# Two adaLN layers with ALiBi attention and mixtures of experts: weights sent in pieces, tile tables and padding moved ahead of a stage boundary, both modulations computed together, and a new order for the uses of a shared PSUM bank

## The chip, the cores and the metric

One core of a Trainium2 chip runs the whole program in one launch. The metric is device time in microseconds, the median over runs. The times stand below beside the profile.

## What is computed

The input is x of shape (32, 256, 128): 32 batch elements of 256 tokens. Each of two layers has its own modulation and then does attention and a mixture of experts. Cut to what matters:

```python
for layer in (0, 1):
    mod = (silu(c) @ wmod).reshape(32, 6, 1, 128)       # c: (32,128), wmod: (128,768)
    sa, ca, ga, sb, cb, gb = mod                        # ga, gb: at least 0.25 in size
    h = layernorm(x) * (1 + ca) + sa
    x = x + ga * attention(h)                           # 16 heads of 8 columns, 256 x 256
    h = layernorm(x) * (1 + cb) + sb
    x = x + gb * experts(h)                             # 8 experts, 128 -> 512 -> 128
# layer 0: attention with a distance bias; top-2 of 8 experts, relu
# layer 1: attention(LN(h)) + LN(h); RMS norm, top-1 of 8 experts, silu, biases b1 and b2
```

Only the chosen experts are computed: tokens are gathered by expert into a buffer in HBM, and each expert's region is worked through in tiles.

## The kernel before, in words

The program is a row of blocks with a barrier over all engines between them: the setup (from L265), `attention(l=0)`, `experts(l=0)`, `attention(l=1)`, `experts(l=1)`. Inside a block every engine has its own instruction list, and semaphores order the engines. SP is the engine that issues the DMAs.

**Setup.** SP issues 24 loads one after another (L293), cT and the two wmod last; then, once VectorE has zeroed the two `stack` buffers (L333), rows of constants into `stack` (L296). ScalarE waits for all loads and takes exp (L312); VectorE finishes silu (L351 to L353); TensorE multiplies (L321, 323, 325). One buffer `mod_sb` holds the rows of one layer's modulation: VectorE shapes layer 0's (L360 to L375), SP writes it to HBM (L299), and only then do TensorE (`if l: pe.wait_ge(moded, 8)`) and VectorE (`dve.wait_ge(mod_out, 16)`) go on with layer 1's. Last SP writes rows of the gates (L301, L303).

**Attention.** `run_ticks` makes 40 ticks; a tick works on several batch elements at once, `at(off)` giving the element that is `off` ahead of or behind the tick's own. In a tick TensorE makes 16 passes `a_pass(h)` of scores for the row maximum (L1173; VectorE takes the maximum, L923, from one of two buffers A), eight `chunk(c)` of scores (L1200, and L1203 in layer 0) for ScalarE's exp (L753), and four `weigh` of probabilities by values (L1218). The second set of scores has the negated row maximum as rows of `stack`: TensorE turns it (`turn_max`, L1180, two halves of eight heads), ScalarE copies it (`max_rows`, L746), SP's DMA puts it into `stack` (`stack_max`, L542). The maximum of half 0 is used from chunk 0 of the next tick, that of half 1 from its chunk 4.

Between these passes TensorE makes small products that share one PSUM bank, M0: `turn_h2` (L1140), `gate` (L1236), `turn_max` (two), `project_v` (L1162), the turns of `On`, `yT` and `xn` (L1140), `project_out` (L1231), and every second tick `count` (L1243, L1246), after which VectorE's `place` gives each token a slot in its expert's region (to L1056) and POOL scatters the tokens (L640). Each use waits (`m0_read`) until the reader of the use before it has read. The order is written out by hand in each engine's `tick`. Ticks with `place` alternate with ticks in which the expert is chosen.

SP sends an attention block's weights for the experts, w1 and w2 (2 MB each, and the biases in layer 1), as whole DMAs ahead of all ticks (L591). In layer 1 `load_front` (L504 to L508) loads the middle x, the experts' outputs and modulation rows, and POOL adds them up (L612).

**Experts.** First SP pads: the tail of the gathered buffer (L1385), then, when VectorE has copied the regions' fill `run` to integers (L1447), eight pads, each at an address read from `run_i` (L1389, L1390). Meanwhile VectorE builds the tables of the tiles (to L1471). When the pads have landed and the table is there, SP loads the first tile (`load_tile`, L1396 and L1399), TensorE turns it (`turn_x`, L1611), and the two products follow (L1620, L1629). Results are scattered by POOL (L1433, L1430).

These lines order one tick of TensorE around `turn_max` before the change:

```python
chunk(2)
a_pass(6)
if at(-1):
    m0_read((logits_read, -3), (h_ready, 1), (mT_read, -1, 1))
    turn_max(*at(-1), 1)
heads_step(weigh, -1, 0)
...
a_pass(15)
if at(0):
    ...
    turn_max(*at(0), 0)
chunk(7)
```

Of the kernel before, what the change touches and what calls it, by code (L numbers as in the profile page):

```python
# [9 lines left out]
ALU = mybir.AluOpType  # L10
AX = mybir.AxisListType

P = 128
# [5 lines left out]
H, HD = 16, 8  # L19
# [114 lines left out]
def build(nc, a, out):  # L134
    with ExitStack() as ctx:
# [6 lines left out]
        def dram(name, shape, dt=F32):  # L142
# [135 lines left out]
            (ln_cols[:, :], a["ln_cols"]), (wv_id[:, :], a["wv_id"]), (gate_w[:, :, :], a["gate_w"]), (cT[:, :, :], a["cT"]),  # L278
            (wmod[:, 0, :], a["wmod0"]), (wmod[:, 1, :], a["wmod1"]),
# [3 lines left out]
        loaded, ready, modp, moded, mod_out = (sem(n) for n in  # L283
            ("setup_loaded", "setup_ready", "setup_products", "setup_modulation", "mod_rows_written"))
        stack_zero, stack_loaded = sem("setup_stack_zeroed"), sem("setup_stack_loaded")
# [3 lines left out]
        with nc.Block() as block:  # L289
            @block.sync  # L290
            def _(sp):
                for dst, src in loads:
                    sp.dma_start(dst, src).then_inc(loaded, 16)  # L293
# [7 lines left out]
                sp.dma_start(gate_rows[:, D:2 * D], mod_sb[:, GA * D:(GA + 1) * D]).then_inc(gates_out, 16)  # L301
                for f in range(2):
                    sp.dma_start(gate_rows[:, f * (D // 2):(f + 1) * (D // 2)].rearrange("b (h d) -> b h d", d=HD),  # L303
                                 mod_sb[:, GA * D:(GA + 1) * D].rearrange("b (h f d) -> b f h d", f=2, d=HD)[:, f, :, :])\
                        .then_inc(gates_out, 16)
                sp.wait_ge(gates_out, 48)
# [3 lines left out]
            def _(act):  # L310
                act.wait_ge(loaded, 16 * len(loads))
# [3 lines left out]
            def _(pe):  # L315
                pe.wait_ge(ready, 1)
                for l in range(2):
                    if l:
                        pe.wait_ge(moded, 8)
                    for j in range(6):  # L320
                        pe.matmul(M0[:, j * B:(j + 1) * B], wmod[:, l, j * D:(j + 1) * D], silu[:, l, :],  # L321
                                  start=True, stop=True)
                    pe.matmul(A[0][0:B, :, :].rearrange("p t s -> p (t s)"), silu[:, l, :], wmod[:, l, 0:512],
                              start=True, stop=True)
                    pe.matmul(A[1][0:B, 0, :], silu[:, l, :], wmod[:, l, 512:768], start=True, stop=True)\
                        .then_inc(modp, 1)
                pe.matmul(M1[:, 0:1], wo[:, :], vo_bias[:, 0:1], start=True, stop=True).then_inc(modp, 1)
# [1402 lines left out]
```

## Time and profile before

| | us |
|---|---|
| median of 3 runs | 2106.24 |
| lowest and highest | 2105.88 and 2109.68 |
| profiled execution, its own time | 2108.88 |
| span of the profiled execution, first to last instruction | 2107.1 |
| mean granted TensorE clock, share of full | 0.923 |

The span falls into these stages, by the barriers in the trace:

| stage | us |
|---|---|
| setup | 0 to 44.9 |
| attention, layer 0 | 44.9 to 795.6 |
| experts, layer 0 | 795.6 to 1095.2 |
| attention, layer 1 | 1095.2 to 1901.8 |
| experts, layer 1 | 1901.8 to 2107.1 |

How to read it: PE is TensorE's products, PEld its weight loads, DVE is VectorE, ACT ScalarE, POOL GpSimd, SPq the queue of SyncE. In a row of the timeline the numbers are the start and the duration in us, and in brackets stands the engine's idle time before the instruction and who ended it. In a row by lines stand the count, the busy time in us, the mean of one in ns, and the idle time before them by what ended it.

### The profile page before, as it was taken

The page shows a single profiled execution, that of the slowest core. Times are in us where ns is not written, and L with a number is a line of the kernel's source. Part 1 is how long each engine was busy: PE and PEld are TensorE (multiplying, and loading weights), DVE is VectorE, ACT ScalarE, POOL GpSimd, SP SyncE. Part 2 cuts the span into 40 slices and gives each one's busy share as a digit, 9 for nine tenths or more (in the row PEclk, how much of TensorE's full clock was granted, in tenths as well). Part 3 has the DMA queues.
Part 4 walks back from the last instruction along what each step waited for, and adds up shares of the span by engine and source line. Part 5 has one row for each costly group of instructions (what it writes and reads, how often), then busy time and mean ns, then how long its engine had stood idle before and what let it go on. Part 6 is the DMA issues. An engine that isn't in the chain of part 4 may idle for free. (4 is left out here: it accounts for less than half of the span.)

```text
span 2107.1 us, 43953 instructions
## 1 busy us (share of the span) xinstructions
PE 1613.4 (77%) x14050; PEld 1155.9 (55%) x14050; DVE 1494.7 (71%) x4845; ACT 1137.7 (54%) x2198; POOL 667.5 (32%) x740
## 2 busy tenths in 40 slices
PE   2488888888888845999963777877877877843996
PEld 1266565656566624999951444444544444523886
DVE  4478888888888734777744787788888788833664
ACT  0277777777677631222211676666666666641543
POOL 0011323232323252555531223233333333230544
PEclk9899999999999977999985898899999999976998
DMA  3333343333333313222235445455455545415443
GB/s 106 85 69 69 79 79 77 79 76 80 77 79 79 67 39 83 72 72 74 72 104 126 85 95 122 97 108 119 102 108 113 109 101 110 91 59 169 133 125 81
DMA packets 267612, 193.24 MB, mean 92 GB/s; under 512 B 26111, under 2 KB 257441, under 8 KB 266612
## 3 DMA queue, kind: packets, MB, share of 16 engines
q1 hardware_dynamic: 252024, 155.41, 35.2%
q0 software_dynamic: 15360, 35.03, 5.4%
q8 instruction: 114, 1.87, 0.4%
q14 instruction: 114, 0.93, 0.2%
HBM read 95.34 MB, written 53.18 MB: 70 GB/s over the span
## 5 line engine op out<-in xcount | busy, mean ns | idle before, releaser
L923 DVE TENSOR_REDUCE mx<-A 128x2 f32<-128x512 f32 x1024 | 688.4, 682 | 213.7 <-PE A L1173 197.3
L753 ACT ACTIVATE probs<-B 128x1024 f32<-128x1024 f32 x512 | 521.8, 1019 | 281.1 <-PE B L1200 154.6
L1173 PE MATMUL A<-stack 126*128 126x256 bf16 x2048 | 398.3, 284 | 113.4 <-DVE mx L923 92.3
L1200 PE MATMUL B<-stack 128*128 128x256 bf16 x2048 | 367.0, 282 | 67.4 <-DMA stack<-mrow 66.7
L1173 PEld LDWEIGHTS A<-stack 126*128 126x128 bf16 x2048 | 169.6, 100 | 266.8 <-DVE mx L923 165.4
L1218 PE MATMUL M<-probs,vals 128*32 128x256 f32 x4096 | 295.1, 408 | 23.8 <-DVE On L946 19.7
L1200 PEld LDWEIGHTS B<-stack 128*128 128x128 bf16 x2048 | 199.4, 102 | 122.3 <-DMA stack<-mrow 82.0
L640 POOL DMA_INDIRECT gathered<-h,slot_in x192 | 186.9, 974 | 128.6 <-DVE slot_in L1056 82.3
L1629 PE MATMUL A<-w2s,hid 128*128 128x128 f32 x1792 | 219.5, 276 | 8.5 <-issue 8.5
L604 POOL TENSOR_TENSOR parts<-rem,parts 128x512 bf16<-128x512 f32 x64 | 74.5, 1165 | 468.1 <-ACT parts L732 468.1
L1629 PEld LDWEIGHTS A<-w2s,hid 128*128 128x128 f32 x1792 | 208.8, 192 | 12.9 <-issue 11.8
L1620 PE MATMUL B<-xtT,w1s 128*128 128x256 f32 x896 | 205.1, 382 | 0.0
L1433 POOL DMA_INDIRECT expert_out<-yt,row_dest x144 | 141.9, 986 | 156.9 <-DVE yt L1536 122.1
L1578 ACT ACTIVATE hid<-B 128x1024 f32<-128x1024 f32 x72 | 73.8, 1025 | 211.8 <-PE B L1620 211.8
L1218 PEld LDWEIGHTS M<-probs,vals 128*32 128x32 f32 x4096 | 120.5, 114 | 116.6 <-issue 75.3
L1203 PE MATMUL B<-dist,slope_ident 128*128 128x128 bf16 x1024 | 183.4, 219 | 0.0
L1620 PEld LDWEIGHTS B<-xtT,w1s 128*128 128x128 f32 x896 | 167.9, 192 | 20.9
L626 POOL TENSOR_TENSOR h<-xn,back_rows 128x256 f32<-128x256 f32 x64 | 46.5, 726 | 366.2 <-ACT xn L691 366.2
L1430 POOL DMA_INDIRECT out<-yt,row_dest x80 | 78.8, 985 | 126.4 <-DVE yt L1533 108.2
L1478 DVE TENSOR_SCALAR w1s<-w 128x512 f32 x112 | 55.5, 495 | 76.2 <-PE B L1620 68.4
L1611 PE MATMUL M<-ident,xt 128*128 128x128 f32 x224 | 43.9, 279 | 81.1 <-DMA xt<-gathered 81.1
L671 ACT ACTIVATE rs<-mv,eps_col 128x2 f32<-128x2 f32 x192 | 55.6, 290 | 93.1 <-DVE mv L849 62.2
(182 smaller groups left out, 2405.5 us busy)
## 6 DMA issues: line engine op xcount, KB each, us to landing
stack<-parts SPq DMA_DIRECT2D x768, 64.0 KB
xt<-gathered SPq DMA_DIRECT2D x112, 132.0 KB, 2.2
probs<-gathered SPq DMA_DIRECT2D x40, 256.0 KB
w<-in_w SPq DMA_DIRECT2D x4, 2048.0 KB, 10.1
back_rows<-mod_rows SPq DMA_DIRECT2D x64, 128.0 KB, 3.7
x_mid<-X SPq DMA_DIRECT2D x64, 128.0 KB, 2.9
hid<-expert_out SPq DMA_DIRECT2D x64, 128.0 KB
X<-in_x SPq DMA_DIRECT2D x32, 128.0 KB, 3.8
```

The source lines that it names most:

```text
L604: pool.tensor_tensor(parts[u][:, :, 2, :], rem[:, :, :], parts[u][:, :, 1, :], ALU.subtract)\
L640: pool.indirect_dma_start(gathered[l], bass.IndirectOffsetOnAxis(ap=place, axis=0), (h3 if l else h2)[:, v, t, :], None).then_inc(scat_out ...
L753: act.activation(probs[c % 4][:, :, :, :], Bp[BUFFER[c]][:, :, :, :], ACT.Exp, scale=EXP_SCALE[l][c // 4]).then_inc(b_exp.handle, 1)
L923: dve.tensor_reduce(mx[u][:, h, :], A[h % 2][:, :, :], AX.X, ALU.max).then_inc(a_max.handle, 1)
L1173: ins = pe.matmul(A[h % 2][:, t, :], stack[u][0:n, h, 0, t * P:(t + 1) * P], stack[u][0:n, h, 1, :], start=True, stop=True)
L1200: ins = pe.matmul(Bp[BUFFER[c]][:, j, t, :], stack[u][:, h, 1, t * P:(t + 1) * P], stack[u][:, h, 0, :], start=True, stop=(l == 1))
L1203: ins = pe.matmul(Bp[BUFFER[c]][:, j, t, t * P:(t + 1) * P], slope_ident[:, h % HH, :], dist[:, :], start=False, stop=True)
L1218: ins = pe.matmul(M1[VW * j:VW * j + VW, 0:S], vals[u][:, t, first:first + VW], probs[(2 * g + j // 2) % 4][:, j % 2, t, :], start=(q == 0 ...
L1430: ins = pool.indirect_dma_start(expert_out[l], dest, yt[s % HELD][:, t, :], None, bounds_check=B * S - 1, oob_is_err=False)
L1433: ins = pool.indirect_dma_start(expert_out[l], dest, yt[s % HELD][:, t, :], None)
L1620: ins = pe.matmul(dst[:, f, :], w1s[u][:, f * P:(f + 1) * P], xtT[u][:, :], start=True, stop=True)
L1629: ins = pe.matmul(A[u][:, t, 0:D], hid[u][:, f, t * P:(t + 1) * P], w2s[u][:, f, :], start=(f == 0), stop=(f == FC - 1))
```

## The change

It does five things.

1. In the setup cT and both wmod are loaded first, with a semaphore of their own; both layers' products, rows and columns have their own places, so that the second waits for nothing of the first; silu stands ahead of VectorE's wait for all loads; POOL instead of VectorE zeroes `stack`.
2. The weights are cut by expert into 16 pieces (18 with the biases), of which SP sends one at the end of each tick from `at(-2)` on.
3. The padding and the tables of the tiles move from the start of the experts' block to the end of the attention block's lists of SP and VectorE. The waits for the table go.
4. `load_front` moves from the end of SP's tick to its start and waits for `h_stats` instead of `h_rows`.
5. The uses of M0 in a tick, and with them steps of ScalarE and VectorE, get a new order: `turn_max` of half 1 stands right behind chunk 0, that of half 0 behind a_pass 10 (layer 1) or a_pass 12 and a turn of heads (layer 0), `project_v` ahead of chunk 3, `count` behind chunk 6, `place` behind the maximum of pass 14.

The diff, cut; first the setup, the weights, the padding and the tables:

```diff
+        first_loads = [(cT[:, :, :], a["cT"]), (wmod[:, 0, :], a["wmod0"]), (wmod[:, 1, :], a["wmod1"])]
+        mods = [mod_sb[:, :], hid[0][0:B, 0:3, :].rearrange("b c s -> b (c s)")]
+        mod_cols = [M0[:, 0:6 * B], M1[:, 0:6 * B]]
...
             def _(sp):
+                for dst, src in first_loads:
+                    sp.dma_start(dst, src).then_inc(first_loaded, 16)
                 for dst, src in loads:
                     sp.dma_start(dst, src).then_inc(loaded, 16)
                 sp.wait_ge(stack_zero, 2)
...
-                    sp.dma_start(mod_rows[l], mod_sb[:, :]).then_inc(mod_out, 16)
-                    sp.wait_ge(mod_out, 16 * (l + 1))
+                    sp.dma_start(mod_rows[l], mods[l]).then_inc(mod_out, 16)
...
-                act.wait_ge(loaded, 16 * len(loads))
+                act.wait_ge(first_loaded, 16 * len(first_loads))
...
-                    if l:
-                        pe.wait_ge(moded, 8)
...
+            @block.gpsimd
+            def _(pool):
+                for u in range(2):
+                    pool.memset(stack[u][:, :, :, :], 0.0).then_inc(stack_zero, 1)
...
-                for u in range(2):
-                    dve.memset(stack[u][:, :, :, :], 0.0).then_inc(stack_zero, 1)
...
-                    dve.wait_ge(modp, l + 1)
-                    if l:
-                        dve.wait_ge(mod_out, 16)
+                    dve.wait_ge(modp, 3 if l else 1)
...
-                    sp.wait_ge(h_rows.handle, h_rows.after(b - 2))
+                    sp.wait_ge(h_stats.handle, h_stats.after(b - 2))
...
-            weights = [(w1[:, :, :], a[f"w1_{l}"]), (w2[:, :, :, :], a[f"w2_{l}"])]
+            weights = [piece for e in range(E) for piece in
+                       ((w1[:, e, :], a[f"w1_{l}"][:, e, :]), (w2[:, e, :, :], a[f"w2_{l}"][:, e, :, :]))]
...
             def tick(at):
+                if l and at(3):
+                    load_front(*at(3))
                 if at(0):
                     stack_up(*at(0), 1)
...
-            for dst, src in weights:
-                sp.dma_start(dst, src).then_inc(weights_in, 16)
+                if at(-2):
+                    for dst, src in itertools.islice(more_weights, 1):
+                        sp.dma_start(dst, src).then_inc(weights_in, 16)
             run_ticks(tick)
...
+                         pads[E:PADS]).then_inc(padded, 16)
+            sp.wait_ge(run_ready, 1)
+            for e in range(E):
+                r = sp.value_load(run_i[0:1, e:e + 1], min_val=e * REGION, max_val=(e + 1) * REGION - TOK)
+                sp.dma_start(gathered[l][bass.ds(r, TOK), :], pads[e]).then_inc(padded, 16)
+            sp.wait_ge(padded, 16 * (E + 1))
             sp.wait_ge(weights_in, 16 * len(weights))
```

ScalarE's and VectorE's order in a tick, and what is added behind VectorE's ticks:

```diff
                 chunk(0)
+                step(max_rows, -1, 1)
...
-                step(max_rows, -1, 1)
                 step(mid_part, 1)
+                step(values, 0)
                 chunk(3)
-                step(values, 0)
...
                 chunk(5)
+                step(max_rows, 0, 0)
...
-                step(max_rows, 0, 0)
                 chunk(7)
...
                 rows(1, rms_moments, -2)
+                maxima(14, 1)
                 group(l, place, -4)
-                maxima(14, 1)
...
             run_ticks(tick)
+            dve.tensor_copy(run_i[:, :], run[:, :]).then_inc(run_ready, 1)
...
```

TensorE's order in a tick:

```diff
                 chunk(0)
+                if at(-1):
+                    m0_read((h_ready, 1), (mT_read, -1, 1))
+                    if not at(1):
+                        counted_before()
+                    turn_max(*at(-1), 1)
                 a_pass(2)
                 heads_step(weigh, -2, 3)
                 if at(-3):
-                    m0_read((h_ready, 1), (mT_read, -1, 1), (mT_read, -2, 2))
+                    m0_read((mT_read, -1, 2), (logits_read, -4))
...
-                if at(-1):
-                    m0_read((logits_read, -3), (h_ready, 1), (mT_read, -1, 1))
-                    turn_max(*at(-1), 1)
                 heads_step(weigh, -1, 0)
                 a_pass(7)
+                if at(0):
+                    m0_read((logits_read, -3), (mT_read, -1, 2), (h_ready, 1))
+                    project_v(*at(0))
                 chunk(3)
-                if at(0):
-                    m0_read((mT_read, -1, 2), (h_ready, 1))
-                    project_v(*at(0))
...
                 a_pass(10)
+                if l:
+                    turn_first_max()
...
                 heads_step(turn_heads, -1, 0)
-                if group_done(at, -4):
...
-                    count(*at(-4))
+                if l == 0:
+                    turn_first_max()
                 a_pass(13)
                 chunk(6)
+                if group_done(at, -4):
+                    m0_read((mT_read, 0, 1), *[(x1_ready, -2)] * (l == 0), (logits_read, -3))
+                    count(*at(-4))
...
                 a_pass(15)
-                if at(0):
-                    ...
-                    turn_max(*at(0), 0)
                 chunk(7)
                 if at(2):
-                    m0_read((mT_read, 0, 1), (h_ready, 1))
+                    if group_done(at, -4):
+                        pe.wait_ge(pos_read.handle, pos_read.after(at(-4)[1]))
+                    else:
+                        m0_read((mT_read, 0, 1), (h_ready, 1))
                     turn(by_tile(xn[at(2)[2]]), xn_ready, at(2)[0], xn_T)
```

In the experts' block the copy of `run`, the tables, the padding and these waits go:

```diff
-            sp.wait_ge(table_ready, 1)
-            sp.wait_ge(zeroed, 16 * (E + 1))
...
-            act.wait_ge(table_ready, 1)
...
-            pe.wait_ge(table_ready, 1)
```

## Rows read from the trace of the kernel before

**Rows 1.** Windows, two attention loops: us; busy us of PE, PEld, DVE, ACT, POOL; PEclk; DMA; GB/s.

```profile
79.20:742.60 663.40, 575.27 (x5958) 396.38 (x5957) 545.25 (x1517) 463.59 (x870) 181.19 (x196) 0.99 0.39 74
1139.60:1852.40 712.80, 554.28 (x4786) 330.14 (x4784) 580.96 (x1812) 471.03 (x958) 217.56 (x264) 0.91 0.50 103
```

**Rows 2.** Timeline of the setup.

```profile
1.67 3.47 DVE L333 MEMSET stack<- 128x4096 uint32 x1 [1.67 <-PEq L1723]
...
16.96 0.26 ACT L312 ACTIVATE silu<-cT 128x64 f32<-128x64 f32 x1 [14.94 <-DMA wmod<-in_wmod]
...
18.54 2.77 PE L321 MATMUL M<-silu,wmod 128*128 128x32 f32 x12 [18.54 <-DVE silu L353]
...
24.04 0.36 DVE L360 COPY modT<-M 128x192 f32<-128x192 f32 x1 [5.56 <-PE A L325]
...
29.45 2.77 PE L321 MATMUL M<-silu,wmod 128*128 128x32 f32 x12 [5.44 <-DVE mod_sb L375]
...
40.02 0.28 DVE L375 SCALAR_TENSOR_TENSOR mod_sb<-mod_sb,qk 32x128 f32<-32x128 f32 x1
...
42.51 0.92 SPq L303 DMA_DIRECT2D gate_rows<-mod_sb  x2
```

**Rows 3.** The page's DMA issues: KB each, us from issue to landing.

```profile
w<-in_w SPq DMA_DIRECT2D x4, 2048.0 KB, 10.1
...
X<-in_x SPq DMA_DIRECT2D x32, 128.0 KB, 3.8
```

**Rows 4.** Timeline, the starts of the two attention blocks.

```profile
59.77 0.49 DVE L858 BATCH_NORM_STATS2 st<-X 128x6 f32<-128x128 f32 x2 [19.12 <-DMA X<-in_x]
...
1114.95 0.72 POOL L612 TENSOR_TENSOR hid<-hid 128x256 f32<-128x256 f32 x1 [25.23 <-DMA gb_row<-mod_rows]
```

**Rows 5.** Timeline, the two boundaries from attention to experts.

```profile
811.43 3.57 SPq L1399 DMA_DIRECT2D xt<-gathered  x3
...
813.78 0.66 PE L1611 MATMUL M<-ident,xt 128*128 128x128 f32 x2 [38.99 <-DMA xt<-gathered]
...
1887.28 0.17 DVE L1056 CAST slot_in<-r 128x4 int32<-128x4 f32 x1
...
1903.96 9.60 SPq L1390 DMA_DIRECT2D gathered<-in_pads  x8
...
1927.20 0.66 PE L1611 MATMUL M<-ident,xt 128*128 128x128 f32 x2 [41.20 <-DMA xt<-gathered]
```

**Rows 6.** PE by lines, 450.7 to 701.5: twelve ticks of layer 0.

```profile
L1200 PE MATMUL B<-stack 128*128 128x256 bf16 x385 | 74.2, 273 | 6.2 <-DMA stack<-mrow 6.2
L1180 PE MATMUL M<-ident_b,mneg 128*16 128x128 bf16 x48 | 6.7, 221 | 3.2 <-DVE lg L1002 3.2
L1140 PE MATMUL M<-ident,On 128*128 128x128 f32 x24 | 5.3, 301 | 8.0 <-ACT vals L739 8.0
```

**Rows 7.** PE by lines, 1449.5 to 1813.5: sixteen ticks of layer 1.

```profile
L1200 PE MATMUL B<-stack 128*128 128x256 bf16 x512 | 83.2, 288 | 21.6 <-DMA stack<-mrow 21.6
L1180 PE MATMUL M<-ident_b,mneg 128*16 128x128 bf16 x64 | 9.2, 228 | 13.8 <-DVE lg L1002 8.6 <-DVE run L1048 5.2
```

**Rows 8.** Windows: two neighbouring ticks of layer 0, two of layer 1.

```profile
492.50:512.00 19.50, 17.99 (x191) 12.57 (x189) 17.25 (x53) 13.84 (x27) 5.96 (x8) 1.00 0.43 81
512.00:534.30 22.30, 18.64 (x198) 12.89 (x197) 17.71 (x49) 16.25 (x31) 7.05 (x8) 1.00 0.36 76
1586.50:1611.00 24.50, 19.93 (x152) 11.50 (x152) 17.77 (x58) 14.57 (x30) 7.48 (x9) 0.80 0.44 106
1611.00:1631.90 20.90, 16.33 (x159) 10.14 (x157) 18.11 (x59) 15.68 (x33) 6.06 (x8) 1.00 0.51 94
```

**Rows 9.** Timeline of POOL and of DVE around 521.9.

```profile
521.81 1.15 POOL L604 TENSOR_TENSOR parts<-rem,parts 128x512 bf16<-128x512 f32 x1 [5.16 <-ACT parts L732]
...
521.88 1.11 DVE L930 TENSOR_SCALAR mneg<-mx 128x16 bf16<-128x16 f32 x1
```

**Rows 10.** Durations of L930 over the span: ns min, median, max.

```profile
L930 DVE TENSOR_SCALAR mneg<-mx x128: 160/175/1148, 86.7 to 1852.5; 128x16 bf16<-128x16 f32 x128
```

More of the change, by code:

```diff
@@ L1 @@
+import itertools
 from contextlib import ExitStack
@@ L343, in _ @@
                 ch.mark(dve.memset(ones_col[:, :, :], 1.0))
+                dve.wait_ge(set_act, 1)
+                ch.link(dve.tensor_scalar(silu[:, :, :], silu[:, :, :], 1.0, None, ALU.add))
+                ch.link(dve.reciprocal(silu[:, :, :], silu[:, :, :]))
+                dve.tensor_tensor(silu[:, :, :], silu[:, :, :], cT[:, :, :], ALU.mult).then_inc(ready, 1)
                 ch.mark(dve.memset(h3[:, :, :, :], 0.0))
@@ L426, in attention @@
         "gb_row ones_col Y expert_out XR a w1 w2 b1 b2".split())
+    tile_iota, run_i, cnt_i, n_tiles, tile_base, reached, tile_tab, tile_e, tile_row, tile_rev = (g[n] for n in
+        "tile_iota run_i cnt_i n_tiles tile_base reached tile_tab tile_e tile_row tile_rev".split())
+    slots = SLOTS[l]
     n_choice = CHOICES[l]
@@ L439, in attention @@
     weights_in, lin_in = sem("weights_in"), sem("lin_in")
+    run_ready, padded = sem("run_ready"), sem("slack_padded")
     def transfers(name, dmas, begun=1, n=2):
@@ L560, in _ @@
                     sp.dma_start(stack[u][BROW:BROW + 2 * NB, :, 0, :], a["no_rows"].bitcast(BF16)).then_inc(lin_in, 16)
+            more_weights = iter(weights)
             for t in (x_in, stack_in, m_in, x1_out, front_in, back_in, x2_out, x2_in, ga_in, gate_in):
@@ L1272, in heads_step, with counted_before, turn_first_max @@
                         step(*at(off), g)
+                def counted_before():
+                    if group_done(at, -5):
+                        pe.wait_ge(pos_read.handle, pos_read.after(at(-5)[1]))
+                def turn_first_max():
+                    if at(0):
+                        m0_read(*[(x1_ready, -2)] * (l == 0), (base_ready if l else v_ready, 0))
+                        turn_max(*at(0), 0)
                 a_pass(0, 1)
                 chunk(0)
+                if at(-1):
[3 more added lines that the diff above has]
+                    turn_max(*at(-1), 1)
                 a_pass(2)
@@ L1278, in tick @@
                 if at(-3):
-                    m0_read((h_ready, 1), (mT_read, -1, 1), (mT_read, -2, 2))
-                    if not at(-1) and group_done(at, -5):
-                        pe.wait_ge(pos_read.handle, pos_read.after(at(-5)[1]))
+                    m0_read((mT_read, -1, 2), (logits_read, -4))
+                    if not at(-1):
+                        counted_before()
                     turn_h2(*held(at, -3))
@@ L1326, in tick @@
                 a_pass(15)
-                if at(0):
+                chunk(7)
+                if at(2):
                     if group_done(at, -4):
```

110 lines of the change are left out of this document (46 added, 64 removed).

## Prediction

> **What bounds the kernel now.** I read the stages first, from the barriers: of 2107.1 us the two attention loops take 663.4 and 712.8 us [rows 1], the experts' loops most of the rest, and around the barriers lie stretches in which the compute engines have next to nothing to do. Then I read the timeline of each such stretch, and last the idle time of TensorE by lines inside the loops.
>
> The setup is one chain: silu starts at 16.96 because it waits for wmod, loaded last; layer 0's products start at 18.54, VectorE's part at 24.04; layer 1's products only at 29.45, their last vector step ends at 40.30, and the gate rows leave at 42.51 [rows 2]. The attention blocks start with VectorE and POOL waiting 19.12 and 25.23 us for their first input [rows 4], the experts' with TensorE waiting 39 and 41 us for the first tile [rows 5].
>
> In the loops no single engine is full. In layer 0 TensorE is busy 18.64 of a 22.30 us tick and VectorE 17.71; in the tick without `place` it is 17.99 and 17.25 of 19.50, so there the two hardly wait. In layer 1 it is 19.93 and 17.77 of 24.50, 16.33 and 18.11 of 20.90 [rows 8]. What is lost are waits of TensorE in its written order: for the row maximum coming back by DMA, for the shared bank's readers, for `vals` [rows 6, 7]. TensorE's granted clock is 0.99 in layer 0's loop, 0.91 in layer 1's [rows 1] and 0.80 in the long tick shown [rows 8]: layer 1, where TensorE waits more, spends part of its time at 1.2 GHz, not 2.4.
>
> **The change part by part.** Gains are negative; the bounds stand in brackets.
>
> *Setup.* With cT and wmod first, three issues take about 1.4 us (0.46 each, the two gate rows' pair [rows 2]). Their landing before: wmod was issued about 12 us in and silu began at 16.96, so 4.9 us; now silu can start near 7.1 and the products 1.6 later, near 8.7. Both layers' products, 5.5 us each (18.54 to 24.04), are done near 19.7. VectorE still waits for all loads (16.96), does 0.7 us of other work, and needs 5.4 us for each layer (24.04 to about 29.4): it ends near 28.5 instead of 40.30. The three gate writes no longer wait for a landing and end near 30.0 instead of 43.4. That is −13.4. POOL's zeroing of `stack` is an operation that this trace doesn't show. VectorE takes 3.47 us for 4096 words [rows 2]; POOL takes 1.15 us for 512 elements of a two-input sum [rows 9], 2.25 ns each, which gives 9.2 us for a buffer, or 18.4 if it goes by two-byte elements. For two buffers that is 7 to 37 us, behind which all of SP's writes queue. Up to 18 us it hides behind the modulation; at 37 SP's nine last issues would end near 43, where they end now. I take −12 [−13.5 to 0].
>
> *First attention block's start.* X was queued behind 4 MB of weights; 2 MB takes 10.1 us to land, X itself 3.8 [rows 3]. Without the weights, X is issued in the block's first microsecond, near 45.5, and VectorE starts at about 49.3 instead of 59.77 [rows 4]: −10.5 [−9.4 to −11]. The pieces are 256 KB, an eighth of 10.1 us or 1.3 us each, one per tick behind `stack_max`. DMA is busy 0.39 and 0.50 of the loops [rows 1], and the next transfer that TensorE waits for comes most of a tick later, so I cost them at 0; were each on the path, 34 pieces would cost 44 us.
>
> *Second attention block's start.* POOL's first sum waits for gb_row, the last of `load_front`'s DMAs, until 1114.95 [rows 4]. Without the weights, SP's first dozen issues at 0.46 us end near 1101 and land 3.8 us later, near 1105: −10 [−8 to −12]. Moving `load_front` to the head of the tick puts it ahead of `stack_up`; `h_stats` comes before `h_rows`, so SP should not stand longer: 0.
>
> *Experts' starts.* Before, tail pad, run copy, eight pads, their landing and then the tile. Now SP starts with `load_tile`. From its issue to TensorE took 2.35 us (811.43 to 813.78 [rows 5]), reading an address about 0.7 (9.60/8 less an issue of 0.46), and SP's first instruction stands some 0.4 behind the barrier. Layer 0: 795.6 + 3.5 = 799.1 instead of 813.78, −14.7 [−13 to −15]. Layer 1: 1905.2 instead of 1927.20, −22. There the moved work may show: the last `place` ends at 1887.45, the eight pads take 9.6 us to issue [rows 5], land by about 1900 to 1901, and the old block's barrier was at 1901.8. The new wait (`padded`) has nothing behind it on SP but the block's end, so it costs 0 to 4; I take −21 [−22 to −17]. In layer 0 TensorE had its last work 38.99 us ahead of 813.78, at 774.8 [rows 5], 21 us ahead of the barrier at 795.6; behind it stands one `place`, and the rest covers some 6 us of tables and 12 of pads.
>
> *Layer 0's loop.* In the twelve ticks TensorE waited 6.2 us for the maximum's DMA, 3.2 at `turn_max` and 8.0 at `On` [rows 6]: 17.4 in six pairs of ticks, 2.9 a pair. Half 0's `turn_max` moves up three to four passes of some 1.2 us, half 1's five; both maxima then land well ahead of their chunks. ScalarE's `values` moves up too, but behind `mid_part`, so the wait for `vals` goes only in part. New waits are `turn_h2` on the second half's copy, the turn of xn on `pos_read`, and `project_v` one chunk earlier; behind each stands TensorE's whole list, and VectorE and ScalarE live on its passes. I bound each by 0 to 0.6 us per tick, about the present wait at `On` (8.0/12). In the tick without `place` VectorE has 2.2 us of slack in all, mostly at the tick's start, and gains little. I take half of 2.9, less a little: −1.3 a pair, times 15.9 pairs (663.4/41.8 [rows 1, 8]), −21 [−8, `turn_max`'s 3.2 alone, to −32].
>
> *Layer 1's loop.* In sixteen ticks 21.6 us for the maximum's DMA and 13.8 at `turn_max` [rows 7], 35.4 in eight pairs or 4.4; with smaller waits at the turns of heads and xn about 5.2, and 15.7 pairs make −82. If the pair only comes down to VectorE's busy time plus the slack that layer 0 has (41.8 − 34.96 = 6.84 [rows 8]), it is 35.88 + 6.84 = 42.7 instead of 45.4, −2.7 or −42. I take the middle, −62 [−28, `turn_max`'s wait alone, to −88]. This includes some of the clock: less waiting means less time at the low level.
>
> The sum: 12 + 10.5 + 21 + 14.7 + 10 + 62 + 21 = 151. The profiled execution took 2108.88, of which 2107.1 is its span and 1.8 lies around it; it is 2.6 above the median 2106.24. Against itself the sum gives 1957.7, against the median 1955. The ends of the sum are 2023 (83 gained) and 1913 (193 gained).
>
> **The rivals.**
> *The loops don't move.* The waits go but TensorE's next one is for VectorE's maxima, busy 17 to 18 us of every tick [rows 8]. Only the boundaries are left: 12 + 10.5 + 14.7 + 10 + 21 = 68, time 2038. Against it: the long ticks leave VectorE 4.6 and 6.7 us of slack. 10%.
>
> *POOL's zeroing stands in VectorE's way.* At 521.81 a POOL instruction of 1.15 us ran; a VectorE step that began 0.07 us later took 1.11 us [rows 9], against a median of 0.175 [rows 10], and both ended within 0.03 us. So an instruction of this kind can be held by POOL. If silu's steps in the setup are held so by a zeroing of 9 to 18 us, the setup's gain goes, time 1967. The Trainium skill ("SBUF — State Buffer", section "Who interferes with whom") has the mechanism: the two engines share a pair of ports as an exclusive lock, held for the whole instruction, and the other "fully blocks"; it also says that a VectorE operation of one input outside the two-port modes is not touched, which is why this stays a rival. By that rule, the row of 1.11 us is the first case. 8%.
>
> *The starts don't do what they say.* The pieces or pads collide with transfers that the loop needs, or new waits hold the block's ends: half of the boundary gain of 56 at the four starts goes, and 10 more is lost in the loops: 1993. 6%.
>
> *Slower: the shared bank becomes the chain.* The new order puts `turn_max` of half 1, `turn_h2`, `gate` and `project_v` close behind each other at the start of the tick, each waiting for a reader on another engine. A wait of the kind at `On` costs 0.67 us; four of them in each of 31.5 ticks of two loops are 2.7 × 63 = 169, and with the boundaries' 68 the time is 2207. It decides from 68/63 = 1.1 us per tick, two such waits that nothing covers. For it: nine uses of one bank in 21 us. Against it: passes and chunks of 1.2 us stand between the uses, and the bank's waits that there are now come to 0.9 us a tick in each layer (3.2 + 8.0 over twelve, 13.8 over sixteen [rows 6, 7]). 3%.
>
> **How the numbers follow.** Forecast 73%, the rivals 10, 8, 6 and 3. The predicted time is 1955. The range is 1915 to 2025: the sum's ends, which take in the second and third rival; the first and the fourth lie above it. Faster by over 0.2% (4 us, about what a measurement of this kernel can tell from no change): 0.96; within it 0.01; slower 0.03.
>
> **What would show it.** Right: products at about 9 us and the barrier near 32; VectorE's first statistics 4 to 5 us behind that; TensorE's first turn 3.5 us behind each experts' barrier; L1200's wait for mrow and L1180's idle time near zero; the granted clock of layer 1's loop above 0.91. Wrong: L1180 or the turn of h2 waiting for ScalarE; xn's turn waiting for `run` in each second tick; VectorE's idle time in the long ticks unchanged; a last block end held by pads; a POOL zeroing that outlasts 30 us.

## The result, and the profile after

The changed kernel takes 1957.28 us (1955.88 to 1961.96, four runs) against 2106.49; the ratio is 0.9293, 95% interval 0.9274 to 0.9311. The forecast was 1955. The profiled execution has a span of 1956.3 us, 150.8 less than before.

ScalarE loads a table at the start of every block, a mark that stands in each trace. From mark to mark (the last stage to the end of the span), in us:

| kernel | setup to | attention 0 | experts 0 | attention 1 | experts 1 |
|---|---|---|---|---|---|
| before | 46.0 | 749.8 | 300.7 | 805.5 | 205.1 |
| changed | 36.6 | 710.2 | 285.4 | 740.3 | 183.8 |
| difference | -9.4 | -39.6 | -15.3 | -65.2 | -21.3 |

Setup of the changed kernel, timeline (start, duration, engine, line; in brackets the idle time before):

```profile
0.75 13.79 POOL L338 MEMSET stack<- 128x8192 bf16 x2 [0.29 <-POOLq L1739]
...
5.74 0.26 ACT L320 ACTIVATE silu<-cT 128x64 f32<-128x64 f32 x1 [3.71 <-DMA wmod<-in_wmod]
6.03 8.55 DVE L354 TENSOR_SCALAR silu<-silu 128x64 f32<-128x64 f32 x1 [2.51 <-ACT silu L320]
...
15.48 2.77 PE L327 MATMUL M<-silu,wmod 128*128 128x32 f32 x12 [15.48 <-DVE silu L356]
...
20.88 2.77 PE L327 MATMUL M<-silu,wmod 128*128 128x32 f32 x12
...
33.01 0.93 SPq L310 DMA_DIRECT2D gate_rows<-hid  x2
```

ScalarE starts 11.2 us earlier than in [rows 2] and both layers' products run back to back. But the first VectorE step of silu, 128x64 numbers, took 8.55 us: it ended at 14.58 with POOL's second zeroing at 14.54. So the gate rows leave at 33.01 instead of 42.51.

The starts of the two attention and the two experts' blocks, timeline:

```profile
39.22 0.49 DVE L877 BATCH_NORM_STATS2 st<-X 128x6 f32<-128x128 f32 x2 [6.70 <-DMA X<-in_x]
...
750.00 0.69 PE L1627 MATMUL M<-ident,xt 128*128 128x128 f32 x2 [25.20 <-DMA xt<-gathered]
...
1039.53 0.72 POOL L631 TENSOR_TENSOR hid<-hid 128x256 f32<-128x256 f32 x1 [13.90 <-DMA gb_row<-mod_rows]
...
1775.71 0.69 PE L1627 MATMUL M<-ident,xt 128*128 128x128 f32 x2 [23.72 <-DMA xt<-gathered]
```

Against [rows 4, 5] the idle time ahead of these is 12.4, 13.8, 11.3 and 17.5 us shorter.

One pair of ticks in each loop, by windows (columns as in [rows 1]):

```profile
333.00:373.00 40.00, 36.76 (x385) 25.49 (x385) 34.59 (x100) 29.69 (x58) 13.03 (x15) 1.00 0.54 95
1517.80:1559.50 41.70, 33.44 (x309) 21.05 (x309) 37.56 (x119) 30.52 (x64) 14.99 (x18) 0.96 0.59 121
```

The pairs in [rows 8] took 41.8 and 45.4 us with the same work; now 40.0 and 41.7. Over the sixteen ticks of [rows 7] and those shown below, a pair of layer 1 went from 45.5 (364.0 / 8) to 42.1 us (336.8 / 8). The granted clock of layer 1's pair is 0.96, against 0.80 and 1.00 in the two ticks of [rows 8]. PE by lines, first twelve ticks of layer 0 (333 to 573.5):

```profile
L1246 PE MATMUL B<-stack 128*128 128x256 bf16 x384 | 73.8, 272 | 0.3 <-ACT probs L772 0.3
...
L1226 PE MATMUL M<-ident_b,mneg 128*16 128x128 bf16 x48 | 6.7, 221 | 1.5 <-ACT hT L733 1.5
...
L1186 PE MATMUL M<-ident,On 128*128 128x128 f32 x24 | 5.3, 300 | 0.0
```

and sixteen ticks of layer 1 (1348.5 to 1685.3):

```profile
L1246 PE MATMUL B<-stack 128*128 128x256 bf16 x512 | 80.6, 281 | 0.2 <-DMA stack<-mrow 0.2
...
L1264 PE MATMUL M<-probs,vals 128*32 128x256 f32 x1024 | 75.8, 412 | 16.6 <-DVE On L965 16.6
...
L1226 PE MATMUL M<-ident_b,mneg 128*16 128x128 bf16 x64 | 8.9, 221 | 3.8 <-ACT hT L733 3.3
...
L1186 PE MATMUL M<-ident,xn 128*128 128x128 f32 x32 | 6.9, 299 | 10.6 <-DVE xn L882 10.5
```

The waits of [rows 6, 7] are gone or small. In layer 1 two others grew: at the turn of xn, in each second tick, from 3.3 us in the sixteen ticks before to 10.6, and at `weigh` from 7.0 to 16.6.

### The profile page after: what moved, and what is told of

The parts are those of the page before. It is cut to its first block and busy times, and to the rows that moved or that the text cites. A ratio compares the mean times of both kernels' runs of the same rounds, so it can differ in the third digit from the quotient of the medians.

```text
span 1956.3 us, 43980 instructions
## 1 busy us (share of the span) xinstructions
PE 1580.6 (81%) x14050; PEld 1151.8 (59%) x14050; DVE 1492.6 (76%) x4843; ACT 1129.0 (58%) x2198; POOL 684.3 (35%) x742
## 5 line engine op out<-in xcount | busy, mean ns | idle before, releaser
L1246 PE MATMUL B<-stack 128*128 128x256 bf16 x2048 | 357.4, 277 | 4.4 <-DMA stack<-mrow 2.8
L1219 PEld LDWEIGHTS A<-stack 126*128 126x128 bf16 x2048 | 160.0, 99 | 288.8 <-DVE mx L942 182.6
L1264 PE MATMUL M<-probs,vals 128*32 128x256 f32 x4096 | 285.5, 395 | 41.6 <-DVE On L965 36.4
L1246 PEld LDWEIGHTS B<-stack 128*128 128x128 bf16 x2048 | 203.8, 101 | 38.9 <-DMA stack<-mrow 4.1
L1249 PE MATMUL B<-dist,slope_ident 128*128 128x128 bf16 x1024 | 183.3, 219 | 0.0
L1599 ACT ACTIVATE hid<-B,b 128x256 f32<-128x256 f32 x160 | 62.8, 475 | 76.6 <-PE B L1636 73.8
L1249 PEld LDWEIGHTS B<-dist,slope_ident 128*128 128x128 bf16 x1024 | 100.3, 98 | 2.7
```

The source lines that it names most:

```text
L1219: ins = pe.matmul(A[h % 2][:, t, :], stack[u][0:n, h, 0, t * P:(t + 1) * P], stack[u][0:n, h, 1, :], start=True, stop=True)
L1246: ins = pe.matmul(Bp[BUFFER[c]][:, j, t, :], stack[u][:, h, 1, t * P:(t + 1) * P], stack[u][:, h, 0, :], start=True, stop=(l == 1))
L1249: ins = pe.matmul(Bp[BUFFER[c]][:, j, t, t * P:(t + 1) * P], slope_ident[:, h % HH, :], dist[:, :], start=False, stop=True)
L1264: ins = pe.matmul(M1[VW * j:VW * j + VW, 0:S], vals[u][:, t, first:first + VW], probs[(2 * g + j // 2) % 4][:, j % 2, t, :], start=(q == 0 ...
```

## The experiments

Twelve kernels ran. All are the changed kernel with one edit, unless it says otherwise. From mark to mark:

| kernel | median | setup to | attention 0 | experts 0 | attention 1 | experts 1 |
|---|---|---|---|---|---|---|
| undo_setup | 1974.60 | 45.1 | 709.2 | 286.6 | 745.9 | 183.3 |
| undo_weights | 1976.37 | 29.8 | 720.5 | 286.7 | 755.0 | 183.8 |
| undo_pads | 1989.44 | 36.7 | 709.5 | 301.3 | 743.1 | 205.6 |
| undo_order | 2029.30 | 29.7 | 741.2 | 286.9 | 781.2 | 183.1 |
| pool_words | 1953.95 | 29.6 | 710.5 | 286.8 | 742.6 | 183.5 |
| front_only | 2092.77 | 45.5 | 748.4 | 301.2 | 786.5 | 205.9 |
| late_max0 | 2033.78 | 29.2 | 740.8 | 286.6 | 789.0 | 183.9 |
| late_max1 | 1948.03 | 29.1 | 711.7 | 285.5 | 737.7 | 183.6 |
| after_again | 1955.28 | 36.6 | 710.4 | 286.3 | 743.4 | 183.9 |
| pads_two | 1959.80 | 29.2 | 710.0 | 286.7 | 748.0 | 183.6 |
| best | 1948.17 | 29.9 | 710.6 | 285.4 | 736.9 | 183.5 |
| half0_only | 2093.62 | 45.4 | 731.4 | 301.0 | 804.9 | 205.5 |

Layer 1's attention varies by itself: 740 to 746 us in kernels that are the same there. Each row of marks is one execution; the medians are over four or five. The expectations below take the setup's end of the changed kernel at the next block's first instruction, 36.4, against the barrier, 44.9, of before; by the mark the difference is 9.4, not 8.5.

**undo_setup:** the setup's code as in before (all of the first part of the diff).

```diff
-                act.wait_ge(first_loaded, 16 * len(first_loads))
+                act.wait_ge(loaded, 16 * len(loads))
...
+                    if l:
+                        pe.wait_ge(moded, 8)
...
-                    pool.memset(stack[u][:, :, :, :], 0.0).then_inc(stack_zero, 1)
...
+                    dve.memset(stack[u][:, :, :, :], 0.0).then_inc(stack_zero, 1)
...
+                    if l:
+                        dve.wait_ge(mod_out, 16)
```

> The changed kernel with the setup as it was before (loads last, one buffer of rows, VectorE zeroing). The stages in the trace of the changed kernel say that the setup's barrier came at 36.4 instead of 44.9: this run should take 8.5 us more than the changed kernel, 1966, if the setup's end is what the first attention block starts from. The rival, that the block's start has slack of its own (its X, or the landing of the rows in stack), gives less than 4 us.

Measured: 1974.60, ratio to before 0.9361 (0.9317 to 0.9406), 17 above the changed kernel. The setup is 8.5 us longer and nothing behind it gives that back; of the rest 5.6 stand in layer 1's attention, which the edit doesn't touch and which lies in its spread.

**undo_weights:** two whole DMAs ahead of the ticks.

```diff
+            weights = [(w1[:, :, :], a[f"w1_{l}"]), (w2[:, :, :, :], a[f"w2_{l}"])]
+            for dst, src in weights:
+                sp.dma_start(dst, src).then_inc(weights_in, 16)
             run_ticks(tick)
```

> The changed kernel with the weights sent whole ahead of the ticks, as before. From the stages: VectorE's first statistics stood 14.9 us behind the barrier and stand 2.8 now, POOL's first sum in layer 1 19.8 and 8.7 now: 12.0 + 11.1 = 23 us, so 1980. The rival, that the 34 pieces cost the loops something that this run gets back (up to 1.3 us each), gives 23 less up to 44, so 1936 to 1978, and shorter steady ticks than the changed kernel's 40.0 and 42.1 us a pair.

Measured: 1976.37, ratio 0.9376 (0.9327 to 0.9426). The attention blocks take 10.3 and 14.7 us more, 25 in all; the setup came out 6.8 us shorter in this execution (see after_again). From the mark to VectorE's first statistics it is 13.9 us instead of 2.7, and to POOL's first sum in layer 1 18.7 instead of 7.4: 11.2 and 11.3, so some 3 of layer 1's 14.7 are its spread. The pairs are 40.0 and about 42.1, as in the changed kernel: the pieces cost the loops nothing.

**undo_pads:** padding and tables back at the start of the experts' block.

```diff
-            sp.wait_ge(padded, 16 * (E + 1))
...
+            sp.wait_ge(table_ready, 1)
+            sp.wait_ge(zeroed, 16 * (E + 1))
```

> The changed kernel with padding and tables of the tiles at the start of the experts' blocks, as before. The first turn of a tile stood 18.2 and 25.4 us behind the barriers and stands 3.5 and 3.4 now, 36.7 in all; SP's wait for the pads (4.3 us) holds the end of layer 1's attention block 4.6 us longer now. Theory: 32 us more than the changed kernel, 1989, and a block end 14.3 us behind the last place in layer 1 instead of 18.9. The rival, that the block's late end has another cause than the pads: 37 us more, and 18.9 stays.

Measured: 1989.44, ratio 0.9425 (0.9378 to 0.9473), 32 above: experts' blocks 15.9 and 21.8 longer. In layer 1 the mark of the next block stands 14.5 us behind the last `place`, not 19.3. So the moved pads do hold that block's end; how is under pads_two.

**undo_order:** TensorE's, ScalarE's and VectorE's order of before.

> The changed kernel with the uses of the shared bank, and ScalarE's and VectorE's steps, in the order of before. By the stages the loops got 28.5 and 58.7 us shorter: if that is all of the new order's doing, this run takes 87 us more, 2044, with pairs of ticks of 41.8 and 45.5 us, TensorE waiting about 0.5 and 1.35 us a tick for the maximum's DMA, and a granted clock of about 0.91 in layer 1's loop. The rival, that the earlier load_front or the weights in pieces did part of it in layer 1: a pair there below 45.5, and less than 75 us more.

```diff
+                if at(-1):
+                    turn_max(*at(-1), 1)
                 heads_step(weigh, -1, 0)
...
                 a_pass(15)
+                if at(0):
+                    turn_max(*at(0), 0)
                 chunk(7)
```

Measured: 2029.30, ratio 0.9631 (0.9582 to 0.9680), 72 above. By the marks 31 us more stand in layer 0, pairs 41.8, the whole gain of that loop, and 41 in layer 1, pairs 44.4 on average and not 45.5, with a setup 6.9 shorter. The rival holds there: part of layer 1's gain comes from elsewhere. The granted clock of layer 1's loop (1105 to 1783) is 0.95, not the 0.91 expected.

**front_only:** the kernel before, with `load_front` moved.

```diff
-                    sp.wait_ge(h_rows.handle, h_rows.after(b - 2))
+                    sp.wait_ge(h_stats.handle, h_stats.after(b - 2))
...
             def tick(at):
+                if l and at(3):
+                    load_front(*at(3))
```

> The kernel before with nothing but load_front's new place and wait. With the old order of the bank the changed kernel had pairs of ticks of about 44.3 us in layer 1, not 45.5, so some 19 us of layer 1's loop came from elsewhere. In the kernel before, POOL's first sum waited 3.7 us a tick for gb_row, the last of load_front's transfers. Theory A (load_front did it): pairs of about 44.3 us, 2087, POOL's wait for gb_row gone. Theory B (the weights in pieces or the shifted phase of the ticks did it): 2106, pairs of 45.5.

Measured: 2092.77, ratio 0.9940 (0.9919 to 0.9961), which is 8 to 17 us and 13 by the medians; by the profiles 19.0 us in layer 1's attention, pairs 44.3 on average. POOL's waits by line in the kernel before (1449.5 to 1813.5; total us, times, longest):

```profile
POOL parts L604 <- ACT parts L732: 100.0, 16, 8.6
POOL hid L612 <- DMA gb_row<-mod_rows: 59.0, 16, 6.7
```

and in front_only (1437 to 1788):

```profile
POOL parts L604 <- ACT parts L732: 146.0, 16, 12.4
```

In front_only the wait for gb_row is not among POOL's. Theory A holds as far as `load_front`'s move does it, with 13 to 19 us. That POOL's waiting was the cost is not shown: of the 59.0 us, 46.0 came back as a longer wait for `parts`.

**half0_only:** the kernel before, with half 0's turn, its copy and `count` moved.

```diff
                 a_pass(10)
+                if l:
+                    turn_first_max()
...
                 heads_step(turn_heads, -1, 0)
+                if l == 0:
+                    turn_first_max()
...
                 chunk(5)
+                step(max_rows, 0, 0)
```

> The kernel before with one part of the new order alone: half 0's turn_max behind pass 10 or 12, its copy behind chunk 5, count behind chunk 6. Undoing this part in the changed kernel cost 76 us, as much as the whole order (72). Theory (this one move carries the order's gain by itself): 2106 less 65 to 80, 2026 to 2041, with pairs of 40.0 to 40.3 us in layer 0 and no wait for the maximum's DMA. Rival (it needs the other moves, or the earlier load_front in layer 1): layer 0 as said, layer 1's pairs 44 or more, 2055 or more.

Measured: 2093.62, ratio 0.9927 (0.9898 to 0.9956). The rival holds in layer 1: nothing there. In layer 0 it is 18.3 us, of the 28.5 of the changed kernel's loop, with pairs of 40.7 and not 40.0 to 40.3. TensorE's wait for the row maxima (L1173) is 11.6 us in six pairs of layer 0 (450.7 to 694.9), against 9.2 in late_max1, where pairs are 40.2; of the moves that late_max1 has and half0_only lacks, that of `place` behind pass 14 is the one that touches these maxima. It was not run by itself. PE by lines in layer 1 (1447 to 1800):

```profile
L1200 PE MATMUL B<-stack 128*128 128x256 bf16 x492 | 80.0, 288 | 23.9 <-DMA stack<-mrow 23.9
```

and the timeline:

```profile
1587.05 0.36 ACT L746 ACTIVATE mrow<-M 16x256 bf16<-16x256 bf16 x1
...
1590.17 0.33 SPq L507 DMA_DIRECT2D front_rows<-mod_rows  x1
1590.55 0.47 SPq L508 DMA_DIRECT2D gb_row<-mod_rows  x1
1591.07 0.69 SPq L542 DMA_DIRECT2D stack<-mrow  x1
...
1595.09 0.61 PE L1200 MATMUL B<-stack 128*128 128x256 bf16 x4 [1.28 <-DMA stack<-mrow]
...
1612.61 0.43 SPq L508 DMA_DIRECT2D gb_row<-mod_rows  x1
1613.08 0.69 SPq L542 DMA_DIRECT2D stack<-mrow  x1
```

The copy of half 0 is ready at 1587.41, but its DMA leaves at 1591.07, right behind `load_front`'s last one, in SP's order. TensorE waits 23.9 us in some 15.4 ticks, 1.55 a tick, for the maximum, no less than the 1.35 of [rows 7].

**late_max0:** half 0's part late again, and `count` ahead of chunk 6 with it.

```diff
-                if l:
-                    turn_first_max()
...
                 a_pass(15)
+                if at(0):
+                    turn_max(*at(0), 0)
                 chunk(7)
```

> The changed kernel with half 0's turn_max back behind pass 15, ScalarE's copy ahead of chunk 7 again, and count ahead of it: the first half of the maximum is late again. If chunk 0's wait for the maximum's DMA was what half 0 cost, TensorE waits about 1 us at every chunk 0 again in layer 0's long ticks and 1.35 us in layer 1, and the time is 20 to 45 us above the changed kernel's, 1977 to 2000. If VectorE's passes bound the ticks anyway, pairs stay at 40.0 and 42.1 and the time below 1965.

Measured: 2033.78, ratio 0.9664 (0.9633 to 0.9695), 76 above the changed kernel and far above the 1977 to 2000 expected. By the marks 31 us more stand in layer 0 and 43 to 49 in layer 1, against its spread of 740 to 746: as much as the whole order. PE by lines in layer 0 (338 to 590):

```profile
L1246 PE MATMUL B<-stack 128*128 128x256 bf16 x384 | 73.9, 273 | 10.1 <-DMA stack<-mrow 10.1
```

The wait for the maximum's DMA is back, 0.84 us a tick.

**late_max1:** half 1's turn behind pass 6, with the old places of `project_v`, `values` and its copy.

```diff
-                    m0_read((h_ready, 1), (mT_read, -1, 1))
-                    turn_max(*at(-1), 1)
...
                 a_pass(6)
+                if at(-1):
+                    turn_max(*at(-1), 1)
```

> The changed kernel with half 1's turn_max back behind pass 6, and with it turn_h2's old waits, project_v behind chunk 3, ScalarE's copy and values in their old places. If the second half carries the other part of the gain (the old order as a whole cost 72 us), this run and the one with half 0 late add up to it: 27 to 52 us here, 1984 to 2009, with TensorE waiting for vals at the turn of On again in layer 0 (0.67 us a tick). If either half alone gives nearly the whole loss, this run is at 2020 or more; if half 0 carries it all, below 1965.

Measured: 1948.03, ratio 0.9260 (0.9225 to 0.9295). No loss: layer 0 1.6 us longer, layer 1 2.6 to 8 shorter. Most of the 9 us under the changed kernel's median are the setup's, whose mark stands 7.4 us earlier (see after_again). PE by lines, layer 0 (333 to 573):

```profile
L1186 PE MATMUL M<-ident,On 128*128 128x128 f32 x24 | 5.3, 301 | 8.0 <-ACT vals L758 8.0
```

The wait at `On` is back in full, 0.67 us a tick, and the pair is 40.2 instead of 40.0. The two halves don't add up: without half 1's part nothing is lost that can be told from chance, so half 0's part carries the gain, together with what late_max1 leaves in place, the moves of `place` and `load_front`.

**pool_words:** four-byte words.

```diff
-                    pool.memset(stack[u][:, :, :, :], 0.0).then_inc(stack_zero, 1)
+                    pool.memset(stack[u][:, :, :, :].rearrange("p h o s -> p (h o s)").bitcast(F32), 0.0).then_inc(stack_zero, 1)
```

> The changed kernel with one line other: POOL zeroes stack as 4096 four-byte words a buffer instead of 8192 two-byte elements. In the changed kernel's trace the two zeroings take 13.8 us, and silu's first VectorE step ran from 6.03 to 14.58, to their end; in the two runs without the new weights or order the same step ended at 7.72, with the first zeroing, and the setup's barrier came 6.9 us earlier, near 29.5. Theory (POOL's zeroing holds VectorE's step, and its time goes by elements): both zeroings end near 7.7, the step ends there in every execution, the barrier comes near 29.5, and the time is 7 us below a disturbed execution of the changed kernel, 1950 to 1951 against its median of 1957. Rival (the time goes by bytes, or the step waits for something else): the zeroing still takes 13.8 us or the step is as long as before; time 1957.

Measured: 1953.95, ratio 0.9286 (0.9260 to 0.9312); the setup's mark at 29.6.

```profile
0.75 6.96 POOL L338 MEMSET stack<- 128x4096 f32 x2 [0.29 <-POOLq L1739]
...
5.85 1.90 DVE L354 TENSOR_SCALAR silu<-silu 128x64 f32<-128x64 f32 x1 [2.34 <-ACT silu L320]
```

Half the elements, half the time; the step ends with the second zeroing again, now at 7.75. The theory holds for the setup. The time is not the 1950 to 1951 expected: the medians differ by less (3 us) than the marks (7), and the intervals overlap.

**after_again:** no edit.

> The changed kernel once more, nothing edited: beside the kernels of this call, and as a second look at its setup. In its first profile silu's VectorE step ended with POOL's second zeroing (14.58) and the barrier came at 36.4; in three edited kernels that have the same setup it ended with the first zeroing (7.7) and the barrier came near 29.5. Theory (which of the two zeroings lets the step go falls out anew in each execution): 36.4 or 29.5 and nothing between, time 1957 or 1950. Rival (it belongs to the program as built): 36.4 again.

Measured: 1955.28, ratio 0.9260 (0.9232 to 0.9288); the step took 8.67 us and the mark is 36.6, as in the first profile. Six edited kernels with the same two zeroings gave: held to the second zeroing in one (undo_pads), released by the first in undo_weights, undo_order, late_max0, late_max1 and pads_two. Two executions of one program agree, which speaks for the rival; each edited kernel was profiled once. The step's own start doesn't decide: 5.91 to 6.03 where it was held to the second, 5.75 to 6.04 where the first let it go. What in a program does stays open.

**pads_two:** half of the pads from ScalarE's queue.

```diff
+            act.wait_ge(run_ready, 1)
+            pad_regions(act, E // 2, E)
```

> The changed kernel with the eight pads shared: four issued by SP, four by ScalarE, which has no work left there. In the changed kernel SP issues them for 9.7 us from 1754.5 and then waits 4.3 us for their landing; the last scatter was issued at 1758.0 and, by the kernel before (barrier 8.8 us behind the last scatter), would have let the block end near 1767.7. Theory: the barrier comes about 4 us earlier, 14.3 to 15 us behind the last place instead of 18.9, the time falls by 4; layer 0 is unchanged (its scatters end later than its pads). Rival (the landing is bound by the bytes, 388 KB each, not by the issues): no change.

Measured: 1959.80, ratio 0.9286 (0.9259 to 0.9313), no gain on after_again. SP's waits at the end of layer 1's attention, for the pads and then at the block's barrier, in the changed kernel and then here:

```profile
SPq L494 <- DMA gathered<-in_pads: 4.3, 1, 4.3
SPq L494 <- PEq L494: 2.4, 1, 2.4
```

```profile
SPq L501 <- DMA gathered<-in_pads: 9.0, 1, 9.0
SPq L501 <- PEq L501: 5.7, 1, 5.7
```

The issues ended after 4.6 us instead of 9.7, and the wait for the landing grew by 4.7. The pads have landed 14.8 us behind the last `place`, 15.3 in the changed kernel: the rival holds for their landing, which the eight times 388 KB set and not the issues. But the mark is not unchanged, as the rival said; it stands 22.1 us behind the last `place`, not 19.3, and SP, done with the pads, waits 5.7 us at the barrier.

The trace points to POOL, whose list ends with a wait for the landing of its scatters. The last packet of their queue ends 7.0 us behind the last `place` in the kernel before and in undo_pads, 10.7 in the changed kernel (up to 11.7 in other kernels with its pads), 14.4 here and 14.5 in best. The mark follows 7.5 to 7.7 us later in before, undo_pads, pads_two and best, and 8.6 in the changed kernel, where the landing of the pads may add the rest. The last scatters of layer 1, median us from issue to landing, in the changed kernel and in best, which shares the pads too:

```profile
gathered<-h,slot_in POOLq DMA_INDIRECT x7, 7.2
```

```profile
gathered<-h,slot_in POOLq DMA_INDIRECT x5, 10.5
```

So the pads sent beside the scatters delay them, here by 3.7 us from one queue and 7.4 from two.

**best:** pool_words, pads_two and, in layer 1 alone, late_max1.

```diff
-                if at(-1):
+                if at(-1) and l == 0:
...
+                if at(-1) and l:
+                    turn_max(*at(-1), 1)
                 heads_step(weigh, -1, 0)
```

> The changed kernel with what the runs so far point to: POOL zeroes in four-byte words, the pads shared by two queues, and in layer 1 alone half 1's turn_max, turn_h2's waits, project_v, values and the copy of half 1 in their old places (with those old in both layers, pairs were 41.2 to 41.5 us in layer 1 instead of 42.1, and 40.2 instead of 40.0 in layer 0). Theory: 7 us or half of it from the setup against the changed kernel's 1957, 8 to 10 from layer 1's loop, 4 from the pads: 1937 to 1943. Rival (the gains overlap, or layer 1's was chance): 1948 to 1953.

Measured: 1948.17 (1946.36 to 1951.09), ratio 0.9232 (0.9208 to 0.9256): faster than before, and by the medians 7 us faster than the changed kernel (after_again, 1953.39 to 1962.55; the intervals of the ratios still overlap). It is not the theory's 1937 to 1943 but the rival's 1948 to 1953. The shared pads lose 3 us instead of gaining 4, which is part of the gap; the rest was not traced, and no run has best without the shared pads. Layer 1's pairs are 41.6 on average, near 41.0 in the last ones.

## Why the prediction was right

*Setup, forecast -12, measured -9.4.* The order of the products came out as described. The step that was mis-sized is silu's start: I had it run free from 7.1, and POOL's zeroing held it to 14.58. That is the second rival, in about half its size: in pool_words, where the step was free at 7.75, the mark stands 7.0 us earlier. POOL's price lay in the bracket: 13.8 us, 0.84 ns an element, not the 2.25 that I took from a two-input sum. The step takes 0.19 us in undo_setup, where nothing runs on POOL; it took 1.7 to 2.0 where it ended with the zeroing that ran when it began, and 8.55 here. The Trainium skill ("SBUF — State Buffer", "Who interferes with whom") says of a VectorE instruction in a two-port mode and one of GpSimd that whoever issues first keeps the shared ports for its whole instruction. The steps of 1.7 to 2.0 us agree with it, and so does pool_words. The 8.55 do not follow from it alone: the step began to wait at 6.03, before POOL's second zeroing began near 7.6, and still sat through that one too.

*Attention's starts, -10.5 and -10, measured* -11.2 *and* -11.1 (from the barriers 14.9 to 3.7 and 19.8 to 8.7); undo_weights gives back 11.2 and 11.3. *Experts' starts, -14.7 and -22, measured -15.3 and -21.3* over the blocks, -14.7 and -22.0 from the mark to the first turn. These terms stood on one wait each, with nothing late behind it.

*Layer 1's block end, 0 to 4 taken as 1, measured 4.6.* With it the term for the second experts' start is -16.7, not -21, just outside its bracket of -22 to -17. I counted the pads' issues, 9.6 us, and two or three for landing, and took nothing to stand behind them but the block's end. Their bytes take longer than their issues, as pads_two shows, and they delay POOL's scatters, for which the block's end waits too: 3.7 of the 4.6 us.

*Layer 0's loop, -21, measured -28.5*, inside the bounds. The mechanism was half right. Half 0's maximum is what mattered most (late_max0 loses all of the gain, half0_only has 18.3 of it). The wait at `On`, 8.0 of the 17.4 us in [rows 6], was worth next to nothing: late_max1 has it in full and loses 1.6 us. TensorE's wait for VectorE's maxima says why, in twelve ticks before, in the changed kernel and in late_max1:

```profile
L1173 PE MATMUL A<-stack 126*128 126x256 bf16 x385 | 73.3, 274 | 11.4 <-DVE mx L923 10.6
```

```profile
L1219 PE MATMUL A<-stack 126*128 126x256 bf16 x385 | 73.6, 274 | 16.3 <-DVE mx L942 13.8 <-DMA stack<-parts 2.2
```

```profile
L1219 PE MATMUL A<-stack 126*128 126x256 bf16 x382 | 72.9, 274 | 9.2 <-DVE mx L942 8.9
```

With the wait at `On` gone, TensorE waits 7.1 us more at its passes than with it (16.3 against 9.2), 4.9 of them for VectorE's maxima. So most of the removed idle time came back, which is what the first rival said of all the waits.

*Layer 1's loop, -62, measured -58.7.* The size is right, the composition isn't. I put all of it on the bank's waits and cost `load_front`'s move at 0, because I asked only what it delays on SP. The move is worth 13 to 19 us by itself (front_only; by which wait is not shown), and it clears the way of `stack_max`, which in SP's order stood behind it, so that half 0's early copy is worth nothing without it (half0_only). Undoing the order costs 41, and the two parts only make the 59 together. The middle between two readings hid an omitted term.

*Clock.* Sixteen ticks of layer 1 by windows, before and then changed (columns as in [rows 1]):

```profile
1449.50:1813.50 364.00, 281.81 (x2468) 168.15 (x2466) 298.45 (x951) 245.09 (x504) 118.60 (x144) 0.92 0.51 108
```

```profile
1348.50:1685.30 336.80, 269.27 (x2472) 169.69 (x2472) 299.63 (x953) 244.54 (x505) 119.78 (x144) 0.95 0.58 122
```

The granted clock rose, as forecast, and the same products take 12.5 us less of TensorE's time. I had tied the rise to the waits that the new order removes; that isn't shown. Over layer 1's whole loop the granted clock is 0.91 before, 0.96 in the changed kernel, and 0.95 in undo_order, where TensorE waits for the maximum's DMA again (15.9 us from 1390 to 1740). These are single executions, and over the whole span the clock of the kernel before varies from 0.91 to 0.93 between executions; in those of undo_order it is 0.93 to 0.94. VectorE's work is the same 299 us of now 337: it is probably what comes next. No run separates the clock's share of the gain from the waits'.

*The other rivals.* The loops did move, 87 us; the starts did what they say; the shared bank did not become the chain. Whether its longer wait at the turn of xn (10.6 us in sixteen ticks) costs anything is not shown; late_max1 has it too, 11.9.

*The sum.* That it came within 3 us is in part luck. Layer 0's loop gave 7.5 us more than its term, and both attention starts with the first experts' start 2.4 more, while the setup gave 2.6 less, layer 1's loop 3.3 less and the second experts' start with the block's end before it 4.3 less.

## What to carry to other kernels

Where a boundary's cost is one wait with one cause, its removal can be priced closely, here to about a microsecond at the four starts; work that moves to the other side of it, as the zeroing and the pads did, needs a price of its own. A loop's idle time is not a sum: here the wait at `On` went and came back, for the most part as a wait for VectorE. When a step moves in an in-order queue, list what it stood ahead of as well as what it now stands ahead of: a transfer made ready early is worth nothing behind a step that waits. A transfer at a block's end has to be priced by its bytes as well as by its issues, and by what it does to the transfers beside it.

## What the runs showed of the hardware that was not expected

POOL's zeroing goes by elements, not bytes: 6.9 us for 8192 two-byte elements a partition, 3.5 for 4096 of four bytes with the same bytes. While two of them are queued, a VectorE step of 0.2 us took 1.7 to 2.0 us where the first one let it through, or 8.6 where only the second did; the same program did the same in two executions, and five of seven programs with this setup did the former.

The last packet of POOL's scatters ended 7.0 us behind the last `place` when no pads were sent beside them, 10.7 us with eight pads of 388 KB from SP's queue, and 14.4 with four each from SP's and ScalarE's, though the pads themselves landed no later.
